# Narrow context attention: turned values, products in four column groups, one output product per unit

## The chip, the cores and the metric

One core of a Trainium2 chip runs the kernel. The metric is device time in microseconds (us). TensorE (PE) multiplies, VectorE (DVE) and ScalarE (ACT) work elementwise, GpSimd (POOL) works on the on-chip memory, and SyncE (SP) starts transfers. PE writes to P, an accumulation memory of eight banks with 512 f32 columns each.

## The reference, cut to what matters

A decoder of four layers, each with an attention, a cross attention to a context of 77 tokens and a feed-forward part; batch 4, 512 tokens, width 128, all f32. Layers 0 and 1 have a cross attention with 16 heads of width 8. In short:

```
q = x @ Wq + bq            # (4, 512, 128)
k = ctx @ Wk + bk          # (4, 77, 128)
v = ctx @ Wv + bv
s = q_head . k_head / sqrt(8)     # layer 1 clamps it
p = softmax(s)                    # (4, 16, 512, 77)
x = layernorm(x + concat_heads(p @ v_head) @ Wo + bo)
```

The product of the shares p and the values v, and then Wo, is what the change touches.

## The kernel before

The kernel is a chain of phases. Each phase gives every engine one instruction stream, written out in order, and the streams meet at semaphores. The function `context_attention` builds four of the phases. With `dh=8` it is called *narrow*; this is so in layer 0 (here **stage A**, about 73 to 196 us of the span) and in layer 1 (**stage B**, about 612 to 755 us, which clamps the scores too). Layers 2 and 3 use other branches of the same function, which stay as they are.

A narrow stage has 16 **units** of 128 tokens (`U = 16`) and four **batches** of four units (`UB = 4`). A unit n goes through these steps:

- `scores(n)`, PE: four products of 308 columns (four heads by 77 tokens) in two halves. Each has 32 rows, so that four lie side by side on the array's row groups. They go to banks 0 to 3.
- `maximum(n, f)`, DVE: the largest value of each head and its subtraction, for each half; in stage B a clamp ahead of it (L1438). Then `exponentials(n)` on ACT, `sums(n, f)` and a reciprocal on DVE, and `shares(n)` on POOL (L1523), which divides.
- `turn(n)`, PE (L1306): the 1232 columns of shares (16 heads by 77) are turned in ten chunks of up to 128, to banks 4 to 6. ACT's `turn(n)` (L1372) copies them to `PT`.
- `result(n)`, PE (L1319): ten products of 128x128 with `VP`, added up in bank 7. DVE's `add(n)` adds the outcome to X.

Per batch, POOL spreads the keys to `KB` and the values to `VB` (L1489: `VB` has 16 copies of the values, each with the rows of one head alone), PE's `keys(b)` makes the queries, and PE's `values(b)` multiplies ten chunks of `VB` with `Wo` (L1278). ACT's `values(b)` copies the outcome, in which Wo is already contained, to `VP`.

Turns run two units behind the scores (`LAG_T`), results three (`LAG_Y`), additions four (`LAG_X`). PE's order in round n is: `scores(n)`, `keys` once in four rounds, `turn(n-2)`, `result(n-3)`, and in rounds 2, 6 and 10 `values` of the next batch. ACT's is: `keys`, `turn(n-2)`, `exponentials(n)`, `values`. Banks 4 to 6 are shared by keys, values and turns. So the list `items` holds all their uses in order, `at` gives the place of each, and a use waits until the use ahead of it has been copied out (semaphore `t_free`). PE signals that one is written with `t_full`.

In rows of TensorE an f32 product shows as two records and a turn as one, so a result shows as x20 and a turn as x10; x4 of L1298 is half a unit's scores and x8 both halves.

Of the kernel before, what the change touches and what calls it, by code (L numbers as in the profile page):

```python
# [16 lines left out]
ACT = mybir.ActivationFunctionType  # L17
# [8 lines left out]
CTX, CD = 77, 96  # L26
# [1143 lines left out]
def context_attention(k, i, c):  # L1170

    nc, P = k.nc, k.P
    w, w_ready = weights(k, i)
    U, UB, H, SC = c.units, c.in_batch, c.heads, c.dh ** -0.5
    ROWS = H * CTX
    LAG_T, LAG_Y, LAG_X = 2, 3, 4
# [15 lines left out]

    items = ["keys 0"]
    for n in range(U + LAG_X):
        items += ["values 0"] * (n == 0)
        items += [f"keys {n // UB + 1}"] * (n % UB == 0 and n // UB + 1 < B)
        items += [f"turn {n - LAG_T}"] * (0 <= n - LAG_T < U)
        items += [f"values {(n - 2) // UB + 1}"] * (n >= 2 and (n - 2) % UB == 0 and (n - 2) // UB + 1 < B)
    at = {name: n for n, name in enumerate(items)}
    with ExitStack() as st, phase(k) as (block, s):  # L1200
# [6 lines left out]
        if c.narrow:  # L1207
            KT, VT = sb("kt", B * CTX), sb("vt", B * CTX)
            KB, VB, QB = sb("kb", 2, 4, CTX), sb("vb", 2, 16, CTX), sb("qb", 2, N)
        else:  # L1210
            KT, VT = sb("kt", c.pairs, B * CTX), sb("vt", c.pairs, B * CTX)
            KB, VM, KP = sb("kb", 2, c.pairs, 2 * CTX), sb("vm", 2, c.pairs, 128), sb("kp", 2, ROWS)
            step = H * LEFT + 2 * LEFT
            VL = sb("vl", 2, c.pairs * step)
# [18 lines left out]
        @block.tensor  # L1233
        def _(pe):
            w_ready(pe)
            for n, o in enumerate(outs):
                kind, p = o[0], int(o[1:] or 0)
                cols = slice(128 * p, 128 * (p + 1))
                if n >= 4:
                    pe.wait_ge(s("prep_a") if n % 2 == 0 else s("prep_v"), n // 2 - 1)  # L1240
                dst = P[:, 4 + n % 4, 0:B * CTX]
                if len(c.segs) == 1:
                    pe.matmul(dst, w["w" + kind][:, cols], k.CT[:, 0, :], start=True, stop=True).then_inc(s("prep"), 1)
                else:
                    pe.matmul(dst, w["w" + kind][:, cols], k.CT[:, 1, :], start=True, stop=False)
                    pe.matmul(dst, w["w" + kind + "i"][:, cols], k.CT[:, 2, :], start=False, stop=True).then_inc(s("prep"), 1)
            pe.wait_ge(s("prep_a"), len(outs) // 2)
            pe.wait_ge(s("prep_v"), len(outs) // 2)

            def keys(b):  # L1250
                if at[f"keys {b}"]:
                    pe.wait_ge(s("t_free"), at[f"keys {b}"])
                if c.narrow:
                    pe.matmul(P[:, 4, :], w["wq"], k.XT[:, N * b:N * (b + 1)], start=True, stop=True).then_inc(s("t_full"), 1)
                    return
                pe.wait_ge(s("built_k"), b + 1)
                each = 3 if H == 16 else 2
                for p in range(c.pairs):
                    last = pe.matmul(P[:, 4 + p // each, 2 * CTX * (p % each):2 * CTX * (p % each + 1)], w["wqt"][:, 128 * p:128 * (p + 1)],
                                     KB[:, b % 2, p, :], start=True, stop=True)  # L1260
                last.then_inc(s("t_full"), 1)

            def values(b):
                pe.wait_ge(s("t_free"), at[f"values {b}"])
                pe.wait_ge(s("built_v"), b + 1)
                for n in range(folded):
                    bk, cols = bank(n)
                    r = rows_of[n]
                    if c.narrow:
                        mms = [(VB[:, b % 2].rearrange("p h j -> p (h j)")[:, 128 * n:128 * n + r], w["wo"])]  # L1270
                    elif n < c.pairs:
                        mms = [(VM[:, b % 2, n, :], w["wo"][:, 128 * n:128 * (n + 1)])]
                    else:
                        h0, hs = left[n - c.pairs]
                        mms = [(VL[:, b % 2, H * LEFT * p + LEFT * h0:H * LEFT * p + LEFT * (h0 + hs)], w["wo"][:, 128 * p:128 * (p + 1)])
                               for p in range(h0 // 2, (h0 + hs + 1) // 2)]
                    for m, (l, r_) in enumerate(mms):
                        last = pe.matmul(P[0:r, bk, cols], l, r_, start=m == 0, stop=m == len(mms) - 1)  # L1278
                last.then_inc(s("t_full"), 1)

            def scores(n):
                b = n // UB
                if n % UB == 0:
                    pe.wait_ge(s("t_free"), at[f"keys {b}"] + 1)
                    if c.narrow:
                        pe.wait_ge(s("built_k"), b + 1)
                for f in range(2):
                    if n:
                        pe.wait_ge(s("sub"), 2 * (n - 1) + f + 1)
                    for m in (2 * f, 2 * f + 1):  # L1290
                        t, h0 = n * c.per + 4 * m // H, 4 * m % H
                        if c.narrow:
                            rows = slice(32 * m, 32 * m + 32)
                            l = QB[rows, b % 2, 128 * (t % QT):128 * (t % QT + 1)]
                            r = KB[rows, b % 2]
                        else:
                            l, r = k.XT[:, 128 * t:128 * (t + 1)], KP[:, b % 2, CTX * h0:CTX * (h0 + 4)]
                        last = pe.matmul(P[:, m, 0:4 * CTX], l, r, start=True, stop=True)  # L1298
                    last.then_inc(s("s_full"), 1)

            def turn(n):
                pe.wait_ge(s("t_free"), at[f"turn {n}"])
                pe.wait_ge(s("shares"), n + 1)
                for m, ch in enumerate(chunks):
                    bk, cols = bank(m)
                    last = pe.transpose(P[0:ch[2], bk, cols], turned(PN[:, n % ED], m), k.ident[:])  # L1306
                last.then_inc(s("t_full"), 1)

            def result(n):
                pe.wait_ge(s("t_free"), at[f"turn {n}"] + 1)  # L1310
                if n % UB == 0:
                    pe.wait_ge(s("t_free"), at[f"values {n // UB}"] + 1)
                if n:
                    pe.wait_ge(s("added"), n)
                for t in range(c.per):
                    mine = [m for m, ch in enumerate(chunks) if ch[0] == t]
                    for m in mine:
                        r = chunks[m][2]
                        last = pe.matmul(P[:, 7, 128 * t:128 * (t + 1)], PT[0:r, n % 2, m, :], VP[0:r, n // UB % 2, chunks[m][3], :],  # L1319
                                         start=m == mine[0], stop=m == mine[-1])  # L1320
                last.then_inc(s("y"), 1)

            keys(0)
            for n in range(U + LAG_Y):
                if n < U:
                    scores(n)
                if n == 0:
                    values(0)
                if n % UB == 0 and n // UB + 1 < B:
                    keys(n // UB + 1)  # L1330
                if 0 <= n - LAG_T < U:
                    turn(n - LAG_T)
                if 0 <= n - LAG_Y < U:
                    result(n - LAG_Y)
                if n >= 2 and (n - 2) % UB == 0 and (n - 2) // UB + 1 < B:
                    values((n - 2) // UB + 1)
# [9 lines left out]
        def _(a):  # L1346
# [26 lines left out]

            def values(b):
                a.wait_ge(s("t_full"), at[f"values {b}"] + 1)
                if b >= 2:
                    a.wait_ge(s("y"), UB * (b - 1))
                whole = [n for n in range(folded) if rows_of[n] == 128]
                last = out_of(VP[:, b % 2], whole, 128)
                for n in range(len(whole), folded):  # L1380
                    last = out_of(VP[:, b % 2], [n], rows_of[n])
                last.then_inc(s("t_free"), 1)

            def turn(n):
                a.wait_ge(s("t_full"), at[f"turn {n}"] + 1)
                if n >= 2:
                    a.wait_ge(s("y"), n - 1)
                last = out_of(PT[:, n % 2], full, 128)
                if len({chunks[m][2] for m in part}) == 1:
# [3 lines left out]
                        last = out_of(PT[:, n % 2], [m], chunks[m][2])  # L1393
                last.then_inc(s("t_free"), 1)

            def exponentials(n):
                for f in range(2):
                    a.wait_ge(s("sub"), 2 * n + f + 1)
# [2 lines left out]

            keys(0)
            for n in range(U + LAG_Y):
                if n == 0:
                    values(0)
                if n % UB == 0 and n // UB + 1 < B:
# [1113 lines left out]
```

## Time and profile before

| | us |
|---|---|
| median of three runs | 2689.15 |
| lowest, highest | 2684.45, 2698.79 |
| profiled execution, its own time | 2677.19 |
| its span, first to last instruction | 2675.4 |
| stage A, from the first query product to the last row mean | 76.2 to 195.7 |
| stage B, the same | 615.6 to 754.6 |

Over the span PE is busy for 79%, DVE 60%, ACT 43% and POOL 28%. These shares are averages over very different phases; for this change only the two stages count. A row of the timeline gives the start, the duration, the engine and the line, and in brackets how long that engine sat idle ahead of it and who released it. The granted TensorE clock is a share of full speed: 1.00 is 2.4 GHz and 0.50 is 1.2 GHz, and a stretch between them was partly at either.

### The profile page before, as it was taken

The page shows a single profiled execution, that of the slowest core. Times are in us where ns is not written, and L with a number is a line of the kernel's source. Part 1 is how long each engine was busy: PE and PEld are TensorE (multiplying, and loading weights), DVE is VectorE, ACT ScalarE, POOL GpSimd, SP SyncE. Part 2 cuts the span into 40 slices and gives each one's busy share as a digit, 9 for nine tenths or more (in the row PEclk, how much of TensorE's full clock was granted, in tenths as well). Part 3 has the DMA queues.
Part 4 walks back from the last instruction along what each step waited for, and adds up shares of the span by engine and source line. Part 5 has one row for each costly group of instructions (what it writes and reads, how often), then busy time and mean ns, then how long its engine had stood idle before and what let it go on. Part 6 is the DMA issues. An engine that isn't in the chain of part 4 may idle for free. (4 is left out here: it accounts for less than half of the span.)

```text
span 2675.4 us, 37100 instructions
## 1 busy us (share of the span) xinstructions
PE 2108.6 (79%) x12720; PEld 1282.2 (48%) x12720; DVE 1606.5 (60%) x3715; ACT 1140.4 (43%) x2176; POOL 743.7 (28%) x914
## 2 busy tenths in 40 slices
PE   6784696776858886997989898685998896678398
PEld 4562573224632324664444454471343565567365
DVE  4676436997957884454555555353565447366687
ACT  2443236653435663223766776332445222233112
POOL 0430002653431100002655556434443000343000
PEclk7796797997968997997999999885799897788599
DMA  1000000001032200002222221103210001000000
GB/s 36 36 1 6 0 1 6 1 0 52 1 96 52 52 1 1 1 1 84 80 80 79 76 76 52 49 1 65 58 41 1 1 1 66 27 1 1 0 1 17
DMA packets 38602, 80.35 MB, mean 30 GB/s; under 512 B 7344, under 2 KB 21680, under 8 KB 37392
## 3 DMA queue, kind: packets, MB, share of 16 engines
q1 hardware_dynamic: 35952, 75.00, 10.2%
q10 hardware_dynamic: 2464, 2.98, 0.4%
q8 instruction: 103, 1.69, 0.3%
q14 instruction: 83, 0.68, 0.1%
HBM read 51.74 MB, written 7.34 MB: 22 GB/s over the span
## 5 line engine op out<-in xcount | busy, mean ns | idle before, releaser
L737 ACT ACTIVATE spt<-P 128x1024 f32<-128x1024 f32 (+3 forms) x256 | 220.8, 863 | 186.1 <-PE P L591 186.1
L704 DVE TENSOR_REDUCE smf<-P 128x2 f32<-128x1024 f32 (+3 forms) x256 | 254.3, 1019 | 47.9 <-PE P L580 23.7
L2268 PE MATMUL P<-XT,W 128*128 128x512 f32 x424 | 220.1, 615 | 63.8 <-ACTq L2302 63.4
L2345 DVE SCALAR_TENSOR_TENSOR X<-P,WE,X 128x128 f32<-128x128 f32 x576 | 162.2, 344 | 147.9 <-PE P L2285 144.6
L2285 PEld LDWEIGHTS P<-W,e_h 128*128 128x128 f32 (+1 forms) x1952 | 220.4, 191 | 60.4 <-issue 51.4
L2285 PE MATMUL P<-W,e_h 128*128 128x128 f32 (+1 forms) x1952 | 227.4, 278 | 3.0 <-DVE X L2345 3.0
L1091 POOL TENSOR_TENSOR d_e<-d_e,d_rc 128x512 f32<-128x512 f32 (+3 forms) x256 | 179.6, 723 | 177.6 <-DVE d_rc L995 147.6
L2313 ACT ACTIVATE e_g<-P 128x512 f32<-128x512 f32 x148 | 88.4, 597 | 320.9 <-PE P L2268 320.9
L1038 ACT ACTIVATE d_e<-d_e,d_mn 128x512 f32<-128x512 f32 (+3 forms) x256 | 141.7, 554 | 131.1 <-DVE d_mn L987 130.7
L2332 DVE TENSOR_TENSOR e_h<-e_g,P 128x512 f32<-128x512 f32 x148 | 101.4, 685 | 108.7 <-PE P L2271 102.8
L2271 PE MATMUL P<-XT,W 128*128 128x512 f32 x296 | 153.9, 602 | 0.0
L1319 PE MATMUL P<-xvp,xpt 128*128 128x128 f32 (+4 forms) x1120 | 144.1, 287 | 11.6 <-DVE X L1463 10.9
L987 DVE CUSTOM_DVE_ANT_0 d_e<-P,d_bt 128x512 f32<-128x512 f32 (+3 forms) x256 | 114.7, 486 | 63.5 <-PE P L919 61.7
L608 PE MATMUL P<-spt,sva 128*32 128x256 f32 (+3 forms) x2048 | 146.1, 363 | 4.5 <-ACT soa L743 2.2
L1319 PEld LDWEIGHTS P<-xvp,xpt 128*128 128x128 f32 (+4 forms) x1120 | 137.7, 202 | 16.0 <-ACT xpt L1372 8.7
L2268 PEld LDWEIGHTS P<-XT,W 128*128 128x128 f32 x424 | 74.5, 196 | 125.0 <-ACTq L2302 63.7
L1455 DVE TENSOR_REDUCE xsm<-xe 128x8 f32<-128x616 f32 (+2 forms) x144 | 88.7, 646 | 75.1 <-ACT xe L1400 72.8
L919 PE MATMUL P<-d_kr,d_qr 64*128 64x256 f32 (+3 forms) x512 | 106.5, 491 | 26.0 <-DVE d_mn L987 25.1
L591 PE MATMUL P<-sqa,ska 64*128 64x512 bf16 (+3 forms) x512 | 94.0, 363 | 40.0 <-ACT spt L737 39.4
L1372 ACT ACTIVATE xpt<-P 117x128 f32<-117x128 f32 (+4 forms) x128 | 73.2, 632 | 113.6 <-PE P L1306 113.6
L909 PEld LDWEIGHTS P<-cst,d_e 128*128 128x128 f32 x640 | 74.5, 144 | 92.4 <-issue 65.8
L909 PE MATMUL P<-cst,d_e 128*128 128x128 f32 x640 | 95.9, 282 | 21.4 <-ACT d_pt L1029 21.4
(376 smaller groups left out, 4170.7 us busy)
## 6 DMA issues: line engine op xcount, KB each, us to landing
d_bt<-in_alibi SPq DMA_DIRECT2D x32, 512.0 KB, 3.7
d_moved<-d_raw SPq DMA_DIRECT2D x256, 64.0 KB, 2.4
ska<-parts_k SPq DMA_DIRECT2D x72, 64.0 KB
sqa<-parts_q SPq DMA_DIRECT2D x72, 64.0 KB
W<-in_w_L_xattn SPq DMA_DIRECT2D x1, 4291.0 KB, 13.9
W<-in_w_L_ffn SPq DMA_DIRECT2D x1, 3333.0 KB, 10.9
W<-in_w_L_ffn SPq DMA_DIRECT2D x1, 3155.0 KB, 10.3
parts_k<-sparts SPq DMA_DIRECT2D x8, 384.0 KB, 2.3
```

What stands on the lines that cost most here:

```text
L608: last = pe.matmul(P[c:c + 32, BANK_PV, cols], VA[:, g // GROUPS % 2, t, (4 * (g % GROUPS) + h) // vrep, :], PT[:, n % 3, h % 2, t, cols], ...
L704: v.tensor_reduce(MF[:, n % 2, u, :], P[:, bank:bank + 2, 0:wide(u)], AX.X, ALU.max, negate=True).then_inc(s("max"), 1)
L737: a.activation(PT[:, n % 3, :, t, N - late(t):N], P[:, BANK_T:BANK_T + 2, 0:late(t)], ACT.Exp, scale=SC).then_inc(s("exp"), 1)
L909: last = pe.transpose(P[:, BANK_T + h, 128 * t:128 * (t + 1)], piece(n, h, u)[:, 128 * t:128 * (t + 1)], k.ident[:])
L987: v.tensor_tensor_reduce(piece(n, h, u), P[:, BANK_S + h, 0:wd], BT[:, n % 4, h, N - wd:N], -SC, 3e38, ALU.add, ALU.min, MN[:, n % 2, u, h ...
L1038: a.activation(piece(n, h, u), piece(n, h, u), ACT.Exp, scale=-1.0, bias=MN[:, n % 2, u, h:h + 1], accum_out=SM[:, n % 2, u, h:h + 1]).the ...
L1091: last = g.tensor_tensor(e, e, RC[:, n % 2, u, h:h + 1].to_broadcast([128, 128 * (u + 1)]), ALU.mult)
L1319: last = pe.matmul(P[:, 7, 128 * t:128 * (t + 1)], PT[0:r, n % 2, m, :], VP[0:r, n // UB % 2, chunks[m][3], :], start=m == mine[0], stop=m ...
L2268: pe.matmul(P[:, PG + j % 2, :], w["w1"][:, col:col + 128], x, start=True, stop=True).then_inc(s("gate"), 1)
L2271: pe.matmul(P[:, PU + j % 2, :], w["w3"][:, col:col + 128], x, start=True, stop=True).then_inc(s("up"), 1)
L2285: last = pe.matmul(P[:, PY + j % 2, 128 * t:128 * (t + 1)], HT[rows, u % 2, blk, 128 * t:128 * (t + 1)], w2, start=n == 0, stop=n == len(p ...
L2345: last = v.scalar_tensor_tensor(x, y, k.WE[:, 4 * c + t, e:e + 1], x, ALU.mult, ALU.add)
```

## The change

Only narrow stages change. `values(b)` no longer multiplies chunks of `VB` with Wo. It turns them with the identity, so that `VP` holds plain values: a row for each pair of head and context token, 128 columns of which only the 8 of its head are not zero. A new step `out(n)` multiplies in the other direction: the stationary operand is 32 columns of `VP` (four heads), the moving one is the turned shares `PT`, and the outcome is 32 rows of bank 4 by 128 tokens. `of_four` lists which chunks hold rows of which four heads: 3, 3, 4 and 3 chunks, which makes 13 products, written round by round over the four column groups. ACT's new `out(n)` copies bank 4 to a new tile `OT`. `projected(n)` is one product of `OT` with Wo to bank 7, and stands where `result(n)` stood. `out(n-3)` comes first in round n on PE and on ACT, ahead of the scores, and enters `items` as a use of the shared banks. What waited for `y` in order to overwrite `PT` or `VP` now waits for the `t_full` of an `out`. DVE's and POOL's streams are the same.

```diff
@@ -1192,6 +1192,7 @@
 
     items = ["keys 0"]
     for n in range(U + LAG_X):
+        items += [f"out {n - LAG_Y}"] * (c.narrow and 0 <= n - LAG_Y < U)
         items += ["values 0"] * (n == 0)
         items += [f"keys {n // UB + 1}"] * (n % UB == 0 and n // UB + 1 < B)
         items += [f"turn {n - LAG_T}"] * (0 <= n - LAG_T < U)
@@ -1207,6 +1208,9 @@
         if c.narrow:
             KT, VT = sb("kt", B * CTX), sb("vt", B * CTX)
             KB, VB, QB = sb("kb", 2, 4, CTX), sb("vb", 2, 16, CTX), sb("qb", 2, N)
+            OT = sb("ot", 2, 128)
+
+            of_four = [[m for m, ch in enumerate(chunks) if ch[1] < 4 * CTX * (g + 1) and ch[1] + ch[2] > 4 * CTX * g] for g in range(4)]
         else:
             KT, VT = sb("kt", c.pairs, B * CTX), sb("vt", c.pairs, B * CTX)
             KB, VM, KP = sb("kb", 2, c.pairs, 2 * CTX), sb("vm", 2, c.pairs, 128), sb("kp", 2, ROWS)
@@ -1267,8 +1271,9 @@
                     bk, cols = bank(n)
                     r = rows_of[n]
                     if c.narrow:
-                        mms = [(VB[:, b % 2].rearrange("p h j -> p (h j)")[:, 128 * n:128 * n + r], w["wo"])]
-                    elif n < c.pairs:
+                        last = pe.transpose(P[0:r, bk, cols], VB[:, b % 2].rearrange("p h j -> p (h j)")[:, 128 * n:128 * n + r], k.ident[:])
+                        continue
+                    if n < c.pairs:
                         mms = [(VM[:, b % 2, n, :], w["wo"][:, 128 * n:128 * (n + 1)])]
                     else:
                         h0, hs = left[n - c.pairs]
@@ -1306,7 +1311,28 @@
                     last = pe.transpose(P[0:ch[2], bk, cols], turned(PN[:, n % ED], m), k.ident[:])
                 last.then_inc(s("t_full"), 1)
 
+            def out(n):
+
+                pe.wait_ge(s("t_free"), at[f"out {n}"])
+                for i_ in range(max(len(g) for g in of_four)):
+                    for g, mine in enumerate(of_four):
+                        if i_ < len(mine):
+                            m = mine[i_]
+                            r = chunks[m][2]
+                            rows = slice(32 * g, 32 * g + 32)
+                            last = pe.matmul(P[rows, 4, 0:128], VP[0:r, n // UB % 2, m, rows], PT[0:r, n % 2, m, :],
+                                             start=i_ == 0, stop=i_ == len(mine) - 1)
+                last.then_inc(s("t_full"), 1)
+
+            def projected(n):
+                pe.wait_ge(s("t_free"), at[f"out {n}"] + 1)
+                if n:
+                    pe.wait_ge(s("added"), n)
+                pe.matmul(P[:, 7, 0:128], OT[:, n % 2, :], w["wo"], start=True, stop=True).then_inc(s("y"), 1)
+
             def result(n):
+                if c.narrow:
+                    return projected(n)
                 pe.wait_ge(s("t_free"), at[f"turn {n}"] + 1)
                 if n % UB == 0:
                     pe.wait_ge(s("t_free"), at[f"values {n // UB}"] + 1)
@@ -1322,6 +1348,8 @@
 
             keys(0)
             for n in range(U + LAG_Y):
+                if c.narrow and 0 <= n - LAG_Y < U:
+                    out(n - LAG_Y)
                 if n < U:
                     scores(n)
                 if n == 0:
@@ -1373,7 +1401,9 @@
 
             def values(b):
                 a.wait_ge(s("t_full"), at[f"values {b}"] + 1)
-                if b >= 2:
+                if b >= 2 and c.narrow:
+                    a.wait_ge(s("t_full"), at[f"out {UB * (b - 1) - 1}"] + 1)
+                elif b >= 2:
                     a.wait_ge(s("y"), UB * (b - 1))
                 whole = [n for n in range(folded) if rows_of[n] == 128]
                 last = out_of(VP[:, b % 2], whole, 128)
@@ -1383,7 +1413,9 @@
 
             def turn(n):
                 a.wait_ge(s("t_full"), at[f"turn {n}"] + 1)
-                if n >= 2:
+                if n >= 2 and c.narrow:
+                    a.wait_ge(s("t_full"), at[f"out {n - 2}"] + 1)
+                elif n >= 2:
                     a.wait_ge(s("y"), n - 1)
                 last = out_of(PT[:, n % 2], full, 128)
                 if len({chunks[m][2] for m in part}) == 1:
@@ -1393,6 +1425,12 @@
                         last = out_of(PT[:, n % 2], [m], chunks[m][2])
                 last.then_inc(s("t_free"), 1)
 
+            def out(n):
+                a.wait_ge(s("t_full"), at[f"out {n}"] + 1)
+                if n >= 2:
+                    a.wait_ge(s("y"), n - 1)
+                a.activation(OT[:, n % 2, :], P[:, 4, 0:128], ACT.Copy).then_inc(s("t_free"), 1)
+
             def exponentials(n):
                 for f in range(2):
                     a.wait_ge(s("sub"), 2 * n + f + 1)
@@ -1401,6 +1439,8 @@
 
             keys(0)
             for n in range(U + LAG_Y):
+                if c.narrow and 0 <= n - LAG_Y < U:
+                    out(n - LAG_Y)
                 if n == 0:
                     values(0)
                 if n % UB == 0 and n // UB + 1 < B:
```

PE's stream around the second values step, before (L1298 scores, L1306 turn, L1319 result, L1278 values):

```order
L1298 MATMUL P<-xkb,xqb 128x308 x4
L1306 MATMUL P<-cst,xe 128x128 x9
L1306 MATMUL P<-cst,xe 80x128
L1319 MATMUL P<-xvp,xpt 128x128 x10
L1278 MATMUL P<-W,xvb 128x128 x9
L1278 MATMUL P<-W,xvb 80x128
L1298 MATMUL P<-xkb,xqb 128x308 x4
```

The same place in the changed kernel (L1303 scores, L1311 turn, L1331 projected, L1274 values, L1323 out):

```order
L1303 MATMUL P<-xkb,xqb 128x308 x4
L1311 MATMUL P<-cst,xe 128x128 x9
L1311 MATMUL P<-cst,xe 80x128
L1331 MATMUL P<-W,xot 128x128
L1274 MATMUL P<-cst,xvb 128x128 x9
L1274 MATMUL P<-cst,xvb 80x128
L1323 MATMUL P<-xpt,xvp 32x128 x13
L1303 MATMUL P<-xkb,xqb 128x308 x4
```

The ten products of the result have gone from behind the turn. One product has taken their place, and thirteen narrow ones stand between the values and the next scores.

## Rows read from the trace of the kernel before

**Rows 1.** The page, its first line.
```profile
span 2675.4 us, 37100 instructions
```

**Rows 2.** Timeline, DVE's first step of neighbouring units, stage A, then B.
```profile
116.40 0.78 DVE L1443 TENSOR_REDUCE xmx<-P 128x8 f32<-128x616 f32 x1
...
122.02 0.78 DVE L1443 TENSOR_REDUCE xmx<-P 128x8 f32<-128x616 f32 x1
...
661.10 0.78 DVE L1438 TENSOR_SCALAR xe<-P 128x616 f32<-128x616 f32 x1
...
668.39 0.78 DVE L1438 TENSOR_SCALAR xe<-P 128x616 f32<-128x616 f32 x1
```

**Rows 3.** Timeline, PE through one unit of stage A, clock at 1.00.
```profile
118.48 0.79 PE L1298 MATMUL P<-xkb,xqb 32*128 32x308 f32 x4
...
120.32 1.31 PE L1306 MATMUL P<-cst,xe 128*128 128x128 f32 x10
121.70 2.47 PE L1319 MATMUL P<-xvp,xpt 128*128 128x128 f32 x20
```

**Rows 4.** Timeline, ACT copying one turn out of P, in two instructions.
```profile
121.67 1.29 ACT L1372 ACTIVATE xpt<-P 128x1152 f32<-128x1152 f32 x2 [1.37 <-PE P L1306]
```

**Rows 5.** Timeline, PE in a later self attention: 128-row, 32-column products on four column groups.
```profile
1019.46 2.37 PE L608 MATMUL P<-spt,sva 128*32 128x256 f32 x40
...
1911.34 0.43 PE L608 MATMUL P<-spt,sva 128*32 128x128 f32 x8
1911.70 0.34 PE L591 MATMUL P<-sqa,ska 64*128 64x384 bf16 x2
```

**Rows 6.** Timeline, PE's values steps 1 and 2 of stage A, 1 to 3 of B.
```profile
98.99 4.26 PE L1278 MATMUL P<-W,xvb 128*128 128x128 f32 x20 [1.38 <-ACT xpt L1372]
...
126.10 4.10 PE L1278 MATMUL P<-W,xvb 128*128 128x128 f32 x20 [1.92 <-POOL xvb L1489]
...
641.26 4.47 PE L1278 MATMUL P<-W,xvb 128*128 128x128 f32 x20 [1.38 <-ACT xpt L1372]
...
673.28 2.39 PE L1278 MATMUL P<-W,xvb 128*128 128x128 f32 x20
...
703.04 2.46 PE L1278 MATMUL P<-W,xvb 128*128 128x128 f32 x20 [1.24 <-POOL xvb L1489]
```

**Rows 7.** Timeline, DVE's restart behind each of these five.
```profile
104.01 0.80 DVE L1443 TENSOR_REDUCE xmx<-P 128x8 f32<-128x616 f32 x1 [2.65 <-PE P L1298]
...
130.96 0.80 DVE L1443 TENSOR_REDUCE xmx<-P 128x8 f32<-128x616 f32 x1 [3.23 <-PE P L1298]
...
646.50 0.80 DVE L1438 TENSOR_SCALAR xe<-P 128x616 f32<-128x616 f32 x1 [1.30 <-PE P L1298]
...
676.43 0.80 DVE L1438 TENSOR_SCALAR xe<-P 128x616 f32<-128x616 f32 x1 [0.27 <-PE P L1298]
...
706.27 0.80 DVE L1438 TENSOR_SCALAR xe<-P 128x616 f32<-128x616 f32 x1 [0.16 <-PE P L1298]
```

**Rows 8.** Timeline, POOL spreading the values ahead of 673.28.
```profile
670.07 2.88 POOL L1489 TENSOR_TENSOR xvb<-xvt,W 128x1232 f32<-128x1232 f32 x1
```

**Rows 9.** Timeline, PE at clock 0.50: half a unit's scores, then a turn.
```profile
633.79 1.40 PE L1298 MATMUL P<-xkb,xqb 32*128 32x308 f32 x4 [3.44 <-DVE xe L1448]
...
667.30 2.40 PE L1306 MATMUL P<-cst,xe 128*128 128x128 f32 x10
```

**Rows 10.** Windows of 5 us: busy us (instructions) of PE, PEld, DVE, ACT, POOL; clock, DMA share, GB/s.
```profile
125.00:130.00 5.00, 3.90 (x20) 3.79 (x20) 2.54 (x7) 0.72 (x1) 3.20 (x2) 0.66 0.01 2
...
165.00:170.00 5.00, 4.59 (x35) 3.33 (x35) 4.78 (x10) 2.34 (x4) 1.62 (x2) 1.00 0.00 0
...
665.00:670.00 5.00, 4.02 (x17) 3.18 (x18) 4.75 (x10) 0.98 (x2) 2.13 (x1) 0.59 0.00 0
```

**Rows 11.** Timeline, stage A's start: PE's first values step, DVE's wait for ACT.
```profile
80.36 3.38 PE L1278 MATMUL P<-W,xvb 128*128 128x128 f32 x20
...
89.03 1.50 DVE L1455 TENSOR_REDUCE xsm<-xe 128x8 f32<-128x616 f32 x2 [5.39 <-ACT xe L1400]
```

## The prediction

> **What bounds the kernel now.** I first laid the two narrow stages out in time, DVE alone, and looked for its idle time. Between two batches there is none. In stage A the first step of a unit starts at 116.40 and of the next at 122.02, in stage B at 661.10 and 668.39 [rows 2]. So a unit costs 5.62 us in A and 7.29 us in B, and DVE's stream sets both. PE beside it: at full clock its unit runs from 118.48 to the end of the result at 124.17, of which 0.79 is half the scores, 1.31 the turn and 2.47 the result [rows 3]. PE is nearly full in A, but scores are ready well ahead of DVE. A shorter result alone is therefore worth nothing there.
>
> The second view was who DVE waits for. It waits at each of the three later `values` steps of a stage, for the first scores behind it [rows 6, 7]. From the start of the values products to DVE's restart it takes 104.01-98.99 = 5.02 us and 130.96-126.10 = 4.86 us in A (the third runs like the second), and 5.24, 3.15 and 3.23 us in B. DVE's waits themselves are 2.65, 3.23 (twice, the third of A being alike) and 1.30, 0.27, 0.16 us, 10.8 us in all. Together with the fill and the drain of a stage this is all that a faster PE could give.
>
> The third view was the granted clock [rows 10]. It is at 1.00 where PE works at its usual pace (165 to 170 us) and fell to 1.2 GHz for part of 125 to 130 us, behind a wait of 1.92 us for POOL. It also fell in 665 to 670 us in stage B, where PE pauses more between units, though PE was busy for 4.02 of 5 us there. At the low level a turn takes 2.40 us instead of 1.31, and half the scores 1.40 instead of 0.79 [rows 9].
>
> **Result replaced by out and projected, 32 units.** The result was 2.47 us [rows 3]. The nearest rows for `out` are products of the same shape, 128 rows by 32 columns, in a later attention [rows 5]: 40 records of 256 columns in 2.37 us. Four of them start together, so these are ten rounds, (2.37-0.40)/9 = 0.22 us apart, with an estimate of 0.40 for the last one's own length (the 8 records of 128 columns take 0.43 in all, start to end); 128 columns take half, 0.11. Thirteen products are 26 records in 8 rounds, since three heads' groups have 3 chunks and one has 4: 7 x 0.11 + 0.30 = 1.07 us. The 0.30 is the rest of those 0.43 us behind one step of 0.11 to 0.13. Bounds: 1.0, and 26 x 0.11 = 2.9 us if the groups did not run beside each other; I take 1.07 since the rows have the very shape. At the low level I scale it as the turn scales, to 1.95 us. `projected` is one product, two records: a fifth of 20 records' time plus its tail, 0.4 us. ACT's added copy of 128 columns takes at most what is left of 1.29 us beside the 1152 columns, about 0.27 us [rows 4]; ACT has room.
>
> PE thus gives up 2.47 and takes on 1.07+0.4, one microsecond a unit. But it is behind DVE, which has no idle time between units, so these 32 us are worth 0.
>
> **What out's place costs.** `out(n-3)` stands ahead of `scores(n)` and waits until the turn of the round before (and, behind a values step, `VP`) has been copied. Scores queue behind it, and DVE waits for scores. The loop of a unit on PE and ACT becomes turn, copy, out, scores: at full clock 1.31+1.33+1.07+0.79 and 0.1 for hand-overs = 4.6 us, under 5.62 and 7.29, cost 0. At the low level it is 2.40+1.33+1.95+1.40+0.1 = 7.2 us. In B that is still hidden by 7.29; in A it costs 7.2-5.62 = 1.6 us for each unit at that level.
>
> **The batch boundaries, six in all.** Before: values products, then scores at once; the copy to `VP` ran beside the scores. After: ten turns, the copy to `VP`, out, scores, in a row. The ten turns take 1.31 or 2.40 us instead of 4.26 or 2.39 [rows 3, 6, 9], but the copy's 1.33 us and the out now lie on the path. The chain is 4.6 us at full clock and 7.2 at the low level. It cannot start earlier by what the result gives up: in A's second boundary PE waited for POOL already, and at 673.28 POOL's values were only ready at 670.07+2.88 = 672.95 [rows 8], so the 3.9 us of the low-clock result there buy 0.3. PE's wait ahead of these steps grows instead by what the result gave up, to 3 or 4 us, and the waits in today's rows already brought the low level. So I take 6.8 us, near the low end. A: 6.8-5.02, 6.8-4.86 twice: +5.7. B: 6.8-5.24, 6.8-0.3-3.15, 6.8-3.23: +8.5. Sum +14.2 (all low: +16.5; all full: +0.9).
>
> The Trainium skill, page "TensorEngine Tiling (Array Packing)", section "PSUM Bottleneck", says that tiling speeds up the products but not the copying out of the accumulation memory, and speaks against this change. The trace agrees as far as the copy's 1.29 us is longer than the 1.07 us of an out. As a bound of throughput it would add nothing to the sum, since ACT is far from full. The same page, "Key Properties", says that a change of the tiling mode drains the engine, and the change adds one per unit. From the last column-group product to the next product of another form, [rows 5] show 1911.70-1911.34 = 0.36 us for two rounds of 0.11, so about 0.1 us; by that rule the sum would grow by 0.6 us at the boundaries.
>
> **The rest.** At the fill of stage A, DVE waited 5.39 us behind the first values step of 3.38 us [rows 11]; ten turns there are over some 1.2 us sooner: -1.2. In B, DVE's own work covers it: 0. At the drain, out, copy and projected with hand-overs (1.07+0.3+0.4) stand for the last result's 2.47: -0.6 to -0.7 a stage, -1.3. Units of A at the low level outside the boundaries: those before the clock rises again, one behind each of one or two boundaries, 1.5 x 1.6 = +2.4. Sum: 14.2-1.2-1.3+2.4 = +14 us. On the profiled execution's 2677.2 us (its span is 2675.4 [rows 1], 1.8 lie around it) this gives 2691; on the median, which is 12 us above that execution, **2703 us**.
>
> **Rivals.**
> - *The clock holds as it does now.* PE's products shrink, but its turns stay. The boundary chains then cost the mean of both ends, (0.9+16.5)/2 = 8.7, and no unit of A is late: 8.7-1.2-1.3 = +6, 2695 us. For it: in most windows the clock is at 1.00. Against: it fell at 665 us with less idle time than the changed kernel will have.
> - *The clock stays low through most of both stages*, the mechanism on the far side. PE works 1 us less in each unit [rows 3, 5], and pauses take its place. If the clock no longer rises between boundaries, the ten units of A that are not at a boundary cost 1.6 each, +16 instead of +2.4, and the boundaries +16.5: 16+16.5-1.2-1.3 = +30, 2719 us. It decides from the point at which pauses of about 1 us in each unit bring the low level. Against: turns keep PE at work.
> - *Faster.* If the clock held at 1.00 and scores got by, the boundaries' waits of 10.8 us and fill and drain's 2.5 us would go: -13, 2676 us. Against: the program order on PE forbids it. Even with the full clock throughout, the terms above give 0.9-1.2-1.3 = -1.6, that is no change.
> - *The column groups do not overlap*: out takes 2.9 us, or 5.8 at the low level, and the loop 4.6-1.07+2.9 = 6.4 us, or 7.2-1.95+5.8 = 11.0. Over 32 units that is 16 x (6.4-5.62) = +12 us at best and 16 x (5.4+3.7) = +146 at worst, about +80, 2769 us. The rows of the same shape speak against it.
>
> **How the numbers follow.** Forecast +14 (from +9 to +20): 0.60. Clock as now or better (+6 down to -2): 0.23. Low clock nearly throughout: 0.12. Faster by waits removed: 0.03. No overlap: 0.02. The range takes in the first three for most of their width: 2691 to 2717 us. A measurement of this kernel can tell about 0.5% from no change, 13.4 us. The forecast lies right at that line, so it gives 0.36 to slower and 0.24 to same; with the rivals: slower 0.36+0.12+0.02 = 0.50, same 0.24+0.23 = 0.47, faster 0.03.
>
> **What would show it.** Right: DVE still at 5.62 and 7.29 us a unit between boundaries; its waits for L1303's scores behind values steps grow to 3 to 5 us; the ACT copy of the turned values ends just ahead of an out, and the scores follow it; out takes 1.1 or 1.9 us; more of both stages at 1.2 GHz. Wrong: boundary chains near 4.6 us, a clock at 1.00 across them, or DVE waiting in every unit. All other phases should stay within noise.

## The result

The changed kernel takes 2700.48 us (median of 22 runs, 2683.72 to 2716.68), the one before 2689.35 us beside it (median of 22 runs, 2667.61 to 2698.79, with one slow run of 3139.05 us among them that is not in the ratio). The ratio is 1.0049, with a 95% interval of 1.0025 to 1.0073: slower by 7 to 20 us, with half a per cent in the middle. The forecast was 2703 us. The sign, the mechanism and the size held. That it met the median within 3 us is in part luck: eleven of the 22 runs lie at 2684 to 2697 us and eleven at 2704 to 2717, so the median falls in a gap where no run is. Several terms inside the forecast were off in both directions, and the experiments show which.

The two profiled executions lie 30.7 us apart (spans 2675.4 and 2706.1 us), so the stages have to be read by themselves. Windows over exactly stage A and stage B, before and then after, show it; the columns are those of [rows 10].

```profile
76.20:195.73 119.53, 97.89 (x696) 77.93 (x696) 86.70 (x160) 52.67 (x79) 52.02 (x25) 0.89 0.04 15
615.56:754.63 139.07, 109.16 (x696) 85.46 (x696) 118.68 (x192) 53.35 (x79) 54.51 (x25) 0.84 0.05 19
```
```profile
76.04:199.93 123.89, 82.31 (x784) 55.81 (x784) 86.65 (x160) 56.25 (x95) 52.04 (x25) 0.84 0.04 14
622.14:769.65 147.51, 96.71 (x784) 64.61 (x784) 118.66 (x192) 56.38 (x95) 54.53 (x25) 0.72 0.04 19
```

A grew by 4.4 us and B by 8.4, together from 258.6 to 271.4 us: **+12.8 us**. The other 17.9 us of the spans' difference lie in phases whose instructions are the same in both, 15.7 us of them behind stage B. That is a difference between executions: in the twelve profiles of this document the part behind stage B takes from 1913 to 1936 us, 1920.8 before and 1936.4 in the changed kernel, and 1913 to 1920 in five kernels that have the changed kernel's code with a small edit. The difference of medians is 11 us. PE is busy for 28 us less in the two stages. DVE's busy time did not move. The granted clock fell from 0.89 to 0.84 in A and from 0.84 to 0.72 in B.

The new steps have the lengths that the self attention's rows promised. One unit of stage A at full clock (the counterpart of [rows 3]):

```profile
145.83 1.31 PE L1311 MATMUL P<-cst,xe 128*128 128x128 f32 x10
146.98 0.39 PE L1331 MATMUL P<-W,xot 128*128 128x128 f32 x2
148.53 1.07 PE L1323 MATMUL P<-xpt,xvp 128*32 128x128 f32 x26 [1.16 <-ACT xpt L1400]
```

Out takes 1.07 us and waits 1.16 us for the copy of the turn; that wait stands where the result's products stood. DVE has no idle time because of it.

The loss is at the boundaries. DVE's restarts there (the counterpart of [rows 7], with the third of A; in the kernel before that one waited 3.21 us):

```profile
104.79 0.80 DVE L1483 TENSOR_REDUCE xmx<-P 128x8 f32<-128x616 f32 x1 [4.71 <-PE P L1303]
134.10 0.80 DVE L1483 TENSOR_REDUCE xmx<-P 128x8 f32<-128x616 f32 x1 [5.42 <-PE P L1303]
163.39 0.80 DVE L1483 TENSOR_REDUCE xmx<-P 128x8 f32<-128x616 f32 x1 [4.98 <-PE P L1303]
655.21 0.80 DVE L1478 TENSOR_SCALAR xe<-P 128x616 f32<-128x616 f32 x1 [3.42 <-PE P L1303]
688.85 0.80 DVE L1478 TENSOR_SCALAR xe<-P 128x616 f32<-128x616 f32 x1 [3.99 <-PE P L1303]
722.51 0.80 DVE L1478 TENSOR_SCALAR xe<-P 128x616 f32<-128x616 f32 x1 [3.98 <-PE P L1303]
```

These waits sum to 26.5 us instead of 10.8. One chain in order of time, all engines, second boundary of A:

```profile
127.05 2.37 PE L1274 MATMUL P<-cst,xvb 128*128 128x128 f32 x10 [3.94 <-POOL xvb L1529]
...
129.45 1.29 ACT L1400 ACTIVATE xvp<-P 128x1152 f32<-128x1152 f32 x2 [2.58 <-PE P L1274]
...
130.79 1.93 PE L1323 MATMUL P<-xpt,xvp 128*32 128x128 f32 x26 [1.38 <-ACT xvp L1400]
...
132.65 1.41 PE L1303 MATMUL P<-xkb,xqb 32*128 32x308 f32 x8
```

PE waits 3.94 us for POOL's values. Then come turns, copy, out and scores, PE's part at the low clock level, and 134.10-127.05 = 7.05 us pass to DVE's restart. From the start of the values step to DVE's restart (called the chain from here on) the six boundaries take 7.07, 7.05, 6.60 and 7.35, 7.05, 7.05 us. PE waits for POOL ahead of four of them. Ahead of the first of each stage it waits 1.38 us for a copy of ACT's, as in the kernel before, and the clock is low there already: 0.50 in each window of 5 us from 90 to 105 us in A, and from 640 to 655 in B.

### The profile page after: what moved, and what is told of

Same layout as the page of the kernel before. It is cut to its first block and busy times, and to the rows that moved or that the text cites. A ratio compares the mean times of both kernels' runs of the same rounds, so it can differ in the third digit from the quotient of the medians.

```text
span 2706.1 us, 37510 instructions
## 1 busy us (share of the span) xinstructions
PE 2100.2 (78%) x12896; PEld 1246.9 (46%) x12896; DVE 1606.0 (59%) x3715; ACT 1148.0 (42%) x2208; POOL 745.2 (28%) x914
## 5 line engine op out<-in xcount | busy, mean ns | idle before, releaser
L704 DVE TENSOR_REDUCE smf<-P 128x2 f32<-128x1024 f32 (+3 forms) x256 | 254.3, 1018 | 53.7 <-PE P L580 30.7
L2385 DVE SCALAR_TENSOR_TENSOR X<-P,WE,X 128x128 f32<-128x128 f32 x576 | 162.1, 344 | 148.6 <-PE P L2325 145.3
L1563 POOL TENSOR_TENSOR xe<-xe,xrc 128x1232 f32<-128x1232 f32 x32 | 72.0, 2249 | 149.4 <-DVE xrc L1518 149.4
L969 DVE TENSOR_TENSOR d_by_cos<-d_raw,W 128x512 f32<-128x512 f32 x64 | 55.6, 870 | 91.9 <-ACT d_raw L1046 91.9
```

Source lines behind the costliest of these rows:

```text
L704: v.tensor_reduce(MF[:, n % 2, u, :], P[:, bank:bank + 2, 0:wide(u)], AX.X, ALU.max, negate=True).then_inc(s("max"), 1)
L2385: last = v.scalar_tensor_tensor(x, y, k.WE[:, 4 * c + t, e:e + 1], x, ALU.mult, ALU.add)
```

## The experiments

Two theories at first. **P** (place): the copy to `VP` and out stand between the values step and the scores. **C** (clock): PE has less to multiply, so the clock falls. Every stage time below is from one profile, first query product to last row mean, as above. One profile also holds chance. The stage's start, which has the same instructions in all kernels with plain values, leaves DVE waiting for 4.16 us in one and 5.36 in another, by when the clock rises, and the last waits of B sum to between 5.4 and 8.6 us. So differences of 1 to 2 us in this table say nothing. The whole kernel's ratios are against the kernel before, and their intervals of about 0.3% either way are wide beside these effects: they tell e2 from the changed kernel, but not e4 from e6, which have the same ratio.

| kernel | A | B | A+B | ratio (95%) |
|---|---|---|---|---|
| before | 119.5 | 139.1 | 258.6 | |
| changed | 123.9 | 147.5 | 271.4 | 1.0049 (1.0025 to 1.0073) |
| e1, out behind all scores | 121.5 | 138.6 | 260.1 | 0.9998 (0.9969 to 1.0027) |
| e2, out behind the scores at boundaries | 117.7 | 136.4 | 254.1 | 0.9966 (0.9933 to 0.9998) |
| e3, before, scores wait for the copy | 125.2 | 142.4 | 267.5 | 1.0036 (1.0003 to 1.0069) |
| e4, changed, 4 idle products a unit | 124.6 | 146.3 | 270.9 | 1.0019 (0.9991 to 1.0047) |
| e5, e2 and e4 | 116.9 | 136.8 | 253.7 | 0.9960 (0.9936 to 0.9983) |
| e6, changed, 12 idle products at boundaries | 117.2 | 142.5 | 259.7 | 1.0019 (0.9991 to 1.0046) |
| e7, out written group by group | 128.9 | 148.6 | 277.5 | one run, no ratio |
| e8, e2 with earlier values | 114.6 | 137.0 | 251.6 | 0.9970 (0.9945 to 0.9994) |
| e9, changed, earlier values | 117.0 | 145.5 | 262.5 | 1.0003 (0.9975 to 1.0032) |
| e10, e2 and e6 | 116.5 | 136.8 | 253.3 | 0.9977 (0.9951 to 1.0003) |

### The place of out: e1 and e2

```diff
-                if c.narrow and 0 <= n - LAG_Y < U:
+                behind = n % UB == LAG_Y and n // UB + 1 < B
+                if c.narrow and 0 <= n - LAG_Y < U and not behind:
                     out(n - LAG_Y)
                 if n < U:
                     scores(n)
+                if c.narrow and behind:
+                    out(n - LAG_Y)
```

This is e2. In e1 out stands behind the scores in every round.

> The changed kernel with out(n-3) behind scores(n) in every round on PE, all else the same. Theory P (the place of out: copy and out ahead of the scores make the boundary chains long): from the start of a values step to DVE's restart it falls from 7.05 us to the turns and the scores, 2.4+1.4 = 3.8 us at the low clock level, so 6 x 3.2 = 19 us less at the boundaries; but each unit's turn now waits for scores, out and its copy (0.8+1.1+0.3 us at full clock, 1.4+1.9+0.3 at the low level), and ACT's exponentials behind the turn's copy come late for DVE: up to 2 us a unit at the low level. Net 7 us below the changed kernel, stages A and B together near 264 us instead of 271.4. Theory C (the loss is the clock, since PE has less to multiply): PE has the same products and as many pauses, so nothing changes: within 2 us of 271.

> The changed kernel with out(n-3) behind scores(n) only in the three rounds per stage that follow a values step. Theory P: the boundary chains fall from 7.05 to about 4 us and no other unit pays: 6 x 2.5 to 3 = 15 to 18 us below the changed kernel in the two stages, 254 to 257 us together, 1 to 4 us below the kernel before. Theory C: within 2 us of the changed kernel's 271.

e2 gives 254.1 us, 17.3 less than the changed kernel and 4.5 less than before, with the same products on every engine. So P holds, and C alone falls. PE and DVE at the third boundary of A in e2:

```profile
155.03 1.28 PE L1274 MATMUL P<-cst,xvb 128*128 128x128 f32 x10 [3.95 <-POOL xvb L1532]
156.24 1.37 PE L1303 MATMUL P<-xkb,xqb 32*128 32x308 f32 x8
157.69 1.93 PE L1323 MATMUL P<-xpt,xvp 128*32 128x128 f32 x26
```
```profile
157.62 0.80 DVE L1486 TENSOR_REDUCE xmx<-P 128x8 f32<-128x616 f32 x1 [0.99 <-PE P L1303]
...
163.26 1.50 DVE L1498 TENSOR_REDUCE xsm<-xe 128x8 f32<-128x616 f32 x2 [2.46 <-ACT xe L1441]
```

The chain is 157.62-155.03 = 2.6 us (3.8 where the clock is low all along). DVE waits 0.99 us instead of 4.98. But the turn that stands behind out comes later, and DVE waits 2.46 us for the exponentials in that unit: a part of the gain is given back one step further on. In e1 such waits for the exponentials come in more units: apart from the stage's start they sum to 17.4 us in the two stages, against 8.8 in e2. That is the main part of why it ends 6 us behind e2, at 260.1 us where 264 was expected.

### The copy alone: e3

```diff
             for n in range(U + LAG_Y):
+                if c.narrow and n % UB == LAG_Y and n // UB + 1 < B:
+                    pe.wait_ge(s("t_free"), at[f"values {n // UB + 1}"] + 1)
                 if n < U:
```

> The kernel before (values folded with Wo, result of ten products), with one wait added: in the three rounds behind a values step the scores wait until ACT has copied the values to VP. This puts the copy alone on the path, with PE's work untouched. Theory P: 1.33 us more at each of six boundaries, less DVE's cover: +8 us in the two stages, 258.6 to 267. Theory C: nothing beyond those 1.33 us, and the clock's stretches stay those of before, so both theories agree on the size; what differs is the share of the changed kernel's loss that this leaves: P says 8 of 13 us are the copy, the rest out itself; C says that under 3 us come from it since DVE has cover.

The stages take 267.5 us, 8.9 more than before (8 expected). Second boundary of B in e3:

```profile
680.91 2.46 PE L1278 MATMUL P<-W,xvb 128*128 128x128 f32 x20 [2.54 <-POOL xvb L1491]
...
683.41 1.29 ACT L1374 ACTIVATE xvp<-P 128x1152 f32<-128x1152 f32 x2 [1.24 <-PE P L1278]
...
684.76 0.80 PE L1298 MATMUL P<-xkb,xqb 32*128 32x308 f32 x8 [1.38 <-ACT xvp L1374]
...
685.59 0.80 DVE L1440 TENSOR_SCALAR xe<-P 128x616 f32<-128x616 f32 x1 [1.61 <-PE P L1298]
```

DVE's waits at the six boundaries grew from 10.8 to 18.8 us. So one copy put on the path at six places, with PE's work untouched, makes some two thirds of the change's 12.8 us. PE waits 1.38 us for it, as it does ahead of out in the changed kernel's chain.

### The clock: e4 and e6

e4 adds four products of the identity ahead of each `projected`, e6 twelve ahead of the later values steps only (at the second and third boundary ahead of the `projected` just before; cut to the lines that matter):

```diff
+            def filler():
+                for _ in range(12):
+                    pe.matmul(P[:, 7, 128:256], k.ident[:], k.ident[:], start=True, stop=True)
...
+                if n in (3, 7):
+                    filler()
...
+                    if c.narrow and n == 2:
+                        filler()
```

> The changed kernel with four products of identity by identity (128x128, 8 records, 0.86 us at full clock) to an unused part of bank 7 ahead of each projected product, work that is not in the reference and whose outcome nobody reads. PE's work per unit is then about that of before, in the order of after. Theory C: the clock holds at 1.00 in more stretches and the two stages lose 7 us or more, 271 to 264 or less, boundary chains at 5 to 6 us. Theory P: the chains are long at full clock too (4.6 us), and at the boundaries PE waits for POOL whatever it did before, so the low level stays there: within 3 us of 271.

> The changed kernel with 12 products of identity by identity (24 records, 2.6 us at full clock, 5.1 at the low level) to an unused part of bank 7 ahead of each later values step, where PE waits for POOL; work that is not in the reference. If the chain's 7.05 us instead of 4.6 are the clock that falls while PE waits, the steps at which the filler still runs at full clock (second and third of A) have chains of 4.6 to 5.5 us and DVE restarts 2 us sooner: A 4 to 5 us under 123.9. In B, where the clock is already low when the filler begins, the filler itself ends late: no gain or up to 2 us lost. If the chain has its length from the copies and products alone, it stays at 7 us.

e4 moved nothing: 270.9 us. PE was busy for 24 us more than in the changed kernel, and B's clock rose from 0.72 to 0.80, but the boundary chains stayed at 7.07, 7.04, 6.63, 7.35, 6.12 and 7.05 us. So in B the low clock between boundaries is nearly free, because DVE covers it: between the boundaries of B, DVE does not wait at all in the changed kernel. In A the filler left the clock at 0.84, so for A e4 tells only that a fuller unit does not shorten the chains. In e6 the clock was held at the one place where PE's products are on the path. PE, e6, at the second boundary of A, and the clock there against the changed kernel's:

```profile
124.13 2.92 PE L1329 MATMUL P<-cst 128*128 128x128 f32 x24
126.88 0.39 PE L1337 MATMUL P<-W,xot 128*128 128x128 f32 x2
128.53 1.28 PE L1274 MATMUL P<-cst,xvb 128*128 128x128 f32 x10 [1.26 <-POOL xvb L1537]
131.19 1.07 PE L1323 MATMUL P<-xpt,xvp 128*32 128x128 f32 x26 [1.38 <-ACT xvp L1408]
132.19 0.80 PE L1303 MATMUL P<-xkb,xqb 32*128 32x308 f32 x8
```
```profile
125.00:130.00 5.00, 3.55 (x31) 3.13 (x29) 4.75 (x10) 2.17 (x5) 3.84 (x3) 1.00 0.02 3
130.00:135.00 5.00, 3.27 (x46) 2.46 (x46) 2.09 (x4) 2.14 (x4) 1.79 (x1) 1.00 0.01 2
```
```profile
125.00:130.00 5.00, 2.37 (x10) 1.96 (x10) 3.45 (x8) 1.59 (x3) 3.84 (x2) 0.66 0.01 2
130.00:135.00 5.00, 4.21 (x39) 2.87 (x40) 0.87 (x2) 1.02 (x3) 0.31 (x1) 0.50 0.01 3
```

PE's wait for POOL is 1.26 us instead of 3.94, and the clock stays at 1.00 through the chain. All six chains are now 4.47 to 4.50 us, where the prediction's full-clock end was 4.6. A falls by 6.7 us (4 to 5 expected), and B by 5.1 against an expectation of no gain or a loss. The clock was indeed low when the filler of B's second boundary began (0.52 from 670 to 675 us), but it rose during the filler. The filler took 3.73 us there and ended with POOL's values just ready, and the chain behind it ran at 1.00. So the expectation for B missed that the filler itself brings the clock up. At the first boundary of each stage PE has little to wait for, and there the filler does end late. In A it takes 4.33 us, and DVE waits as long as without it (4.71 us):

```profile
98.29 4.33 PE L1329 MATMUL P<-cst 128*128 128x128 f32 x24
102.45 1.25 PE L1274 MATMUL P<-cst,xvb 128*128 128x128 f32 x10
```
```profile
106.92 0.80 DVE L1491 TENSOR_REDUCE xmx<-P 128x8 f32<-128x616 f32 x1 [4.68 <-PE P L1303]
```

C is a factor after all, at the four later boundaries not through the lighter load of a unit but through PE's wait ahead of the boundary. These gains are read from one profile; the whole kernel's ratio of e6 does not show them clear of noise.

Of a chain of 7.05 us, then, 2.55 us are the clock. Copy and out ahead of the scores cost 2.45 us more at full clock (4.5 against 2.05 in e10) and 3.3 at the low level (7.1 against 3.8 in e2). The two factors overlap, because out's own products are slower at the low level too, so their gains cannot be added.

### Where the chain starts: e9 and e8

```diff
-                if n % UB == 1 and 0 < n // UB < B - 1:
+                if n % UB == (0 if c.narrow else 1) and 0 < n // UB < B - 1:
                     build_values(n // UB + 1)
```

> The changed kernel with POOL spreading the values of the next batch one unit earlier (behind shares(4) and shares(8) instead of shares(5) and shares(9)), all else the same. Theory S (POOL's late values set when four of the six boundary chains start, and PE's wait of 3 to 4 us there brings the low clock): PE's waits for xvb of 3.94, 3.95, 3.83 and 2.99 us go, the chains start that much earlier and run nearer to the full-clock 4.6 us than to 7.05; two boundaries a stage have 3 to 5 us less, 12 to 18 us in all, the two stages 254 to 259 us instead of 271.4. Rival (the chain is long by its products and copies alone, the clock falls by PE's lighter load): the chains start earlier but stay at 7 us, and the gain is what starts earlier minus nothing, still 10 or more, but the measured chain length tells the two apart: 4.6 to 5.5 against 7.

> e2's order (out behind the scores only in the round after a values step) with POOL's values one unit earlier. If place and start are the two causes, DVE has no wait left at the second and third boundary of a stage: e2's 254.1 us less about 2 x (3.2+2.5) us in A and little in B, where DVE's cover is larger: 245 to 250 us, and the whole kernel 8 to 14 us under the one before (ratio 0.995 to 0.997). If the loss at those boundaries is DVE's own work, nothing changes against e2.

e9 gained 8.9 us (12 to 18 expected), most of it in A. Of this 1.1 us is chance: the first boundary of A, which the edit does not reach, took 6.00 us instead of 7.07. The other chains stayed long: 7.12 and 6.39 us in A, 7.42 twice in B, where 4.6 to 5.5 was expected. PE in e9:

```profile
127.92 1.31 PE L1274 MATMUL P<-cst,xvb 128*128 128x128 f32 x10 [1.04 <-ACT xpt L1400]
131.87 1.93 PE L1323 MATMUL P<-xpt,xvp 128*32 128x128 f32 x26 [2.64 <-ACT xvp L1400]
```
```profile
129.92 0.72 ACT L1438 ACTIVATE xe<-xe 128x616 f32<-128x616 f32 x1 [0.82 <-DVE xe L1488]
130.54 1.27 ACT L1400 ACTIVATE xvp<-P 128x1152 f32<-128x1152 f32 x2
```

The turns start sooner and at full clock, but out waits 2.64 us for the copy instead of 1.38: ACT's stream has the exponentials of the round ahead of `values`, and these wait for DVE. During this new wait the clock falls again (0.83 from 130 to 132 us, 0.50 from 132 to 134), and out takes 1.93 us. So theory S holds for the start but not for the chain's length, by which it was to be told from its rival: a second wait had been right behind the first, and e9 alone does not part the two. In e8 the scores do not wait for that copy; A falls to 114.6 us, the shortest of all, B stays at e2's level, as its cover by DVE is larger. 251.6 us is 7 under the kernel before (245 to 250 expected).

### The order of the column groups: e7

```diff
-                for i_ in range(max(len(g) for g in of_four)):
-                    for g, mine in enumerate(of_four):
+                for g, mine in enumerate(of_four):
+                    for i_ in range(max(len(g) for g in of_four)):
```

> The changed kernel with out's 13 products written group by group instead of round by round over the four column groups. If the gain of the groups lies in neighbouring products on different groups, they no longer overlap: out takes 26 x 0.11 = 2.9 us at full clock instead of 1.07, 5.6 at the low level instead of 1.93, the loop of a unit 6.4 to 11 us, and the two stages some 60 to 140 us longer than 271. If PE reorders them, out stays near 1.1 us.

```profile
108.58 1.81 PE L1323 MATMUL P<-xpt,xvp 128*32 128x128 f32 x26 [1.16 <-ACT xpt L1400]
```

Out takes 1.81 us, neither 1.07 nor 2.9. Group by group, the end of one group still runs beside the start of the next: the trace's single records step by 0.11 us within a group, six to eight of them, and the four groups begin at 0, 0.25, 0.50 and 0.96 us. The stages cost 6 us more, against 60 to 140 expected.

### Both remedies: e10 and e5

> e2's order (out behind the scores in the round after a values step) together with e6's filler of 12 products of identity by identity ahead of each later values step (work that is not in the reference, read by nobody). Theory: place and clock are two factors of one chain, 2.4+1.4 us in e2 and 1.3+0.8+1.33+1.07 in e6. Both at once leave 1.3+0.8+0.4 = 2.5 us at full clock, so A comes to 114 to 116 us and B to 134 to 138, together 250 to 252 against e2's 254.1 and e6's 259.7; the kernel is 6 to 9 us under the one before (ratio near 0.997). If the filler's own length in B at the low level eats it, B stays at 136 to 140 and the sum at e2's 254.

> e2's order with four products of identity by identity ahead of each projected product (as in e4; work that is not in the reference). e4 alone moved the two stages by 0.5 us. If the low clock costs only at the boundaries, and there because of PE's wait for POOL, it moves nothing here either: within 3 us of e2's 254.1. If the clock between boundaries matters once the order is right (B had 65 us at the low level in e2), B falls by 2 us or more.

e10's chains are 2.01 to 2.99 us, about the 2.5 expected. The second boundary of A:

```profile
130.77 1.28 PE L1274 MATMUL P<-cst,xvb 128*128 128x128 f32 x10 [1.25 <-POOL xvb L1540]
...
132.81 0.80 DVE L1494 TENSOR_REDUCE xmx<-P 128x8 f32<-128x616 f32 x1 [0.42 <-PE P L1303]
```

But the two stages take 253.3 us (250 to 252 expected) against e2's 254.1, which is no difference in single profiles. Once DVE's wait at a boundary is near 1 us or nothing, a shorter chain has nothing left to give; the exponentials behind it now decide. e5 agrees, 253.7. Neither is a kernel to keep, since the idle products do no work. **e2 and e8** are: all their products belong to the computation, and both are below the changed kernel and the one before, e8 at 2674.27 us against 2682.45 in its own comparison. Their intervals end at 0.9998 and 0.9994, so the gain over the kernel before is small and just clear of noise. Which of the two is better can't be told by them.

## Why the prediction was right

**What bounds the kernel.** Right. DVE's busy time is unchanged, and a unit's pace with it. The microsecond that PE saves per unit brought nothing.

**The new steps.** Out 1.07 and 1.93 us (forecast 1.07 and 1.95), projected 0.39 to 0.46 (0.4), ACT's copy of out 0.28 (0.27). The Trainium skill, page "TensorEngine Tiling (Array Packing)", section "PSUM Bottleneck", says that copying out may become the limit behind tiled products. That holds here in latency and not in throughput: in e3 the copies alone cost 8.9 us, while ACT was busy for only 107 of 268 us (113 of 271 in the changed kernel).

**The boundary chains.** Forecast 6.8 us each and +14.2 in sum. Measured 7.03 us in the mean, and DVE's waits grew by 26.5-10.8 = 15.7 us. The term was slightly too small, because the low level covered nearly the whole chain; only the third of A had turns in 1.92 instead of 2.4 us. Its reason, the longer wait of PE for POOL (3.94 instead of 1.92 us) that brings the low level, is shown by e6 for the four later boundaries. At the first of each stage no result stands ahead of the values step and nothing was given up: the level was low there before PE's wait, so the forecast of 6.8 us fits these two for another reason.

**The rest.** The fill gave 5.39-4.27 = 1.1 us (forecast 1.2). The drain gave 1.3 us in A and 1.2 in B by DVE's last waits (6.7 to 5.4, 9.3 to 8.1), 2.5 instead of 1.3: mis-sized, in B because one old result ran at the low level there, 4.61 us; for A the cause of the larger gain stays open. The 2.4 us for low-level units in A were mis-sized the other way. Outside boundaries, fill and drain, DVE's waits in A only went from 3.0 to 3.7 us, so this term was 0.7: behind a boundary the clock rose during the next unit's turn (1.97 us behind the first of A). These errors nearly cancel: 15.7-1.1-2.5+0.7 = 12.8, the measured sum. So it is in part luck that 14 came so near 12.8. The small terms are also less sure than they look: DVE's wait at the fill was 5.36 us in e1 and e8, with the same instructions there as in the changed kernel, by which the fill would have given nothing.

**The rivals.** *The clock holds* was out: it fell to 0.84 and 0.72. *Low clock through both stages* was out as well: A was low for a third of its time and B for over half (1.00-0.72, of which 0.50 would be all of it), but in B this costs almost nothing between boundaries, where DVE never waits; the estimated loop of 7.2 us fits under 7.29. The *faster* rival was right on what forbids the gain: e2 lifted exactly that order and gained 17.3 us. Its price of -13 us against the kernel before was not reached: e2 came to -4.5 and e8 to -7.0, as new waits for the exponentials took the place of the old ones. The *no overlap* rival was over-priced too: even group by group, out takes 1.81 us.

**The line between same and slower.** The forecast put +14 us at the limit of 13.4 and gave slower 0.50. The ratio's middle is 0.49%, right at that line, so this was as undecided as the text said; the 22 runs of each kernel put it clear of no change all the same.

## What to carry to other kernels

An in-order engine should first do the work that another engine waits for. Ask what is queued behind each new wait before asking how long the new work is; here moving one step behind the scores in six places was worth more (17.3 us) than the change had cost (12.8). A wait of TensorE ahead of a critical chain can be paid twice, once as time and once as a low clock in the chain, as at four boundaries here. And what put the copy of `VP` on the path was not that the values became plain, but that its first user was moved ahead of the scores: e2 keeps the plain values and is 4.5 us under the kernel before in the two stages.

## What was not expected of the hardware

The column groups overlap even without a round-robin order, in part: 26 records of 128 columns took 1.81 us group by group and 1.07 us round by round. A few products that compute nothing, put where TensorE would wait for 3.9 us, brought or kept the granted clock at 1.00 and shortened the chains behind them from 7.03 to 4.49 us in the mean. In one profile of each, that is a net gain of 11.7 us over the changed kernel's two stages. Where TensorE had little to wait for, at the first boundary of A, the same products gained nothing.
